# Feed-forward weights quantised and the rows of batches 0 to 11 normalised and transposed inside the first attention

## The reference

```python
x = x + jnp.tanh(g_xattn[0]) * _L0_xattn_ref(_layernorm(x, axis=-1), ctx_1024, ...)   # 16 heads of 64
x = x + jnp.tanh(g_ffn[0]) * _L0_ffn_ref(_layernorm(x, axis=-1), w_gate, w_up, w_down)

def _L0_ffn_ref(x, w_gate, w_up, w_down):
    x = act_qdq(x)                                # 16 bits, ONE scale: max |x| over all rows / 32767
    up = act_qdq(x @ lpbq_dequant(w_up).T)        # weights 4 bits, a scale for each 32 of a row
    gate = act_qdq(x @ lpbq_dequant(w_gate).T)
    sig = fixed_qdq_u16(jax.nn.sigmoid(gate))
    gate = act_qdq(gate * sig)
    o = act_qdq(gate * up)
    return o @ lpbq_dequant(w_down).T
```

## Time and profile before

| | |
|---|---|
| median of three runs | 1631.07 us (1628.36 to 1631.30) |
| profiled execution, its own time | 1624.04 us |
| its span | 1622.2 us |
| TensorE busy | 1399.8 us, 86% |
| DVE busy | 1230.6 us, 76% |
| ACT busy | 1103.1 us, 68% |
| GpSimd busy | 179.3 us, 11% |
| mean granted clock of TensorE | 0.936 |

### The profile page before, as it was taken

The page is one execution under the profiler, slowest core; times in us unless marked ns, Lnnn a source line. Parts: engine busy times, 40 slices in busy tenths (PEclk is TensorE's granted clock), DMA queues, the critical chain, the costliest instruction groups (busy, mean ns, idle before and its releaser), DMA issues. The chain is left out here.

```text
span 1622.2 us, 40480 instructions
## 1 busy us (share of the span) xinstructions
PE 1399.8 (86%) x15436; PEld 995.7 (61%) x15436; DVE 1230.6 (76%) x3108; ACT 1103.1 (68%) x2440; POOL 179.3 (11%) x177
## 2 busy tenths in 40 slices
PE   5899999999999993492379898989898689999996
PEld 3577666666667662340366666666666367788884
DVE  5888888888888877758778999898898877344443
ACT  5777777777777763467428889888888654366663
POOL 1000001100000002200000000000000100034443
PEclk9999999999999997797688999999999889999998
DMA  6122232332322211000011121211010072122221
GB/s 206 46 86 85 85 107 90 96 107 85 98 93 91 76 60 59 0 1 26 0 57 50 54 77 54 77 51 28 18 35 12 21 251 68 56 35 46 49 45 23
DMA packets 64924, 105.67 MB, mean 65 GB/s; under 512 B 7449, under 2 KB 38914, under 8 KB 63586
## 3 DMA queue, kind: packets, MB, share of 16 engines
q1 hardware_dynamic: 58018, 94.83, 18.6%
q0 software_dynamic: 6720, 8.27, 3.2%
HBM read 68.88 MB, written 35.11 MB: 64 GB/s over the span
## 5 line engine op out<-in xcount | busy, mean ns | idle before, releaser
L1482 ACT ACTIVATE a_p<-a_s,a_nb 112x375 f32<-112x375 f32 x256 | 140.9, 598 | 26.5 <-DVE a_nb L1585 26.2
L271 PE MATMUL a_ps_o<-a_vh,a_pt 125*128 125x64 f16 (+1 forms) x1536 | 152.8, 183 | 2.6 <-ACT a_pt L1495 0.8
L1402 PE MATMUL a_ps_t<-ident,a_p 112*128 112x112 f32 x768 | 118.1, 284 | 42.6 <-ACT a_p L1482 41.3
L273 PE MATMUL a_ps_o<-a_vh,a_pt 125*128 125x64 f16 (+1 forms) x1536 | 151.1, 182 | 0.0
L272 PE MATMUL a_ps_o<-a_vl,a_pt 125*128 125x64 f16 (+1 forms) x1536 | 151.0, 182 | 0.0
L618 ACT ACTIVATE a_p<-a_ps_s,a_nb 112x375 f32<-112x375 f32 x256 | 144.0, 573 | 2.7 <-DVE a_scaled L768 2.1
L271 PEld LDWEIGHTS a_ps_o<-a_vh,a_pt 125*128 125x128 f16 x1536 | 133.5, 98 | 14.7 <-ACT a_pt L1495 6.4
L626 ACT ACTIVATE a_pt<-a_ps_t 125x336 f16<-125x336 f32 x256 | 101.5, 448 | 59.4 <-PE a_ps_t L555 59.1
L1402 PEld LDWEIGHTS a_ps_t<-ident,a_p 112*128 112x128 f32 x768 | 79.6, 146 | 97.8 <-issue 82.7
L272 PEld LDWEIGHTS a_ps_o<-a_vl,a_pt 125*128 125x128 f16 x1536 | 130.8, 98 | 11.0 <-issue 0.2
L1585 DVE CUSTOM_DVE_ANT_0 a_s<-a_s,a_fill 112x375 f32<-112x375 f32 x256 | 130.3, 547 | 5.5
(11 more groups left out here) (443 smaller groups left out, 4486.7 us busy)
## 6 DMA issues: line engine op xcount, KB each, us to landing
a_piece<-in_w SPq DMA_DIRECT2D x72, 256.0 KB, 3.0
split_weights<-a_pair SPq DMA_DIRECT2D x72, 256.0 KB, 3.3
w<-split_weights SPq DMA_DIRECT2D x8, 1024.0 KB, 6.1
a_ctx<-in_ctxT SPq DMA_DIRECT2D x16, 375.0 KB, 3.6
ctx<-a_cx SPq DMA_DIRECT2D x16, 375.0 KB, 4.2
a_cx<-ctx SPq DMA_DIRECT2D x16, 375.0 KB, 5.9
w1h<-split_weights SPq DMA_DIRECT2D x2, 1792.0 KB, 14.8
w1l<-split_weights SPq DMA_DIRECT2D x2, 1792.0 KB, 18.0
```

The source lines that it names most:

```text
L271: nc.tensor.matmul(out, wh, mh, start=(i == 0), stop=False)
L273: last = nc.tensor.matmul(out, wl, mh, start=False, stop=(i == n - 1))
L1402: mm = nc.tensor.matmul(ps_t[:, 2 * (g % 2) + i, t * S:(t + 1) * S], p32[:, g % 2, i, t * KV:t * KV + 128], ident32[0:S, 0:S], start=(t == ...
L1482: nc.scalar.activation(p32[:, g % 2, i, 0:NC], s2[:, g % 2, i, :], ACT.Exp, bias=nb[:, g % 2, i:i + 1], scale=-1.0).then_inc(exp_done, 1)
```

## The change

- `norm_phase` and `WeightQuantiser` go, and with them the block.
- `xh` and `xl` become one tile `x16` with the two halves of a group of four batches side by side, so that the room of a group (`row_floats`) can hold the normalised rows in fp32 once the attention's queries are done with it. `of_batch` gives a batch's columns.
- The weights are quantised in six parts i of 768 columns in the attention: `block_scales` in slot 2, `block_steps` in slot 3 and `block_values` in slot 6 of the batches 2, 3, 5, 6, 7 and 10, all on DVE (GpSimd and ACT had a part of it before), and 14 T jobs in slots 3 and 6 of batches 3, 4, 6, 7, 8, 10, 11 and 12. SP loads part i in its iteration `QUANT_AT[i]` - 1 into the room of the attention's weight stage, two parts deep.
- `bn_stats` of the finished row b - 1 stands in slot 5 of batch b. The rows of batches 0 to 11 are normalised from batch 13 on (`FLAT_ROW_AT`), with six N jobs (`FLAT_AT`), whose results stay fp32; DVE finds the largest of each.
- The feed-forward's own block begins with the last four rows, the largest of all, the all-reduce and the scale; then ACT rounds to 16-bit integers, and DVE makes the two fp16 halves, a cast and a subtraction for each part of a group, 16 in all; TensorE starts as soon as the first group is split.

```diff
+        QUANT_AT = {0: 2, 1: 3, 2: 5, 3: 6, 4: 7, 5: 10}
+        T_AT = {(3, 3): ("T0", 0), (3, 6): ("T1", 0), (4, 3): ("T0", 1), (4, 6): ("T1", 1), (6, 3): ("T0", 2),
+                (6, 6): ("T1", 2), (7, 3): ("T0", 3), (7, 6): ("T1", 3), (8, 3): ("T0", 4), (8, 6): ("T1", 4),
+                (10, 3): ("T2", 4), (11, 3): ("T0", 5), (11, 6): ("T1", 5), (12, 3): ("T2", 5)}
+        FLAT_AT = {NP * b + p: (f"N{k}", n) for n, (b, ps2) in enumerate(((14, (1, 2)), (14, (7, 8)), (15, (5, 6))))
+                   for k, p in enumerate(ps2)}
+        FLAT_ROW_AT = {NP * b + p + i: TG * n + i for n, (b, p) in enumerate(((13, 4), (14, 3), (15, 1))) for i in range(TG)}
...
+            def load_quant(i):
+                src, o = quant_source(i)
+                if i == 0:
+                    sp.wait_ge(w_lo, len(loads))
+                if i >= 2:
+                    sp.wait_ge(q_rounded, i - 1)
+                sp.dma_start(raw[:, i % 2, :].rearrange("p (o d) -> p o d", o=o), src).then_inc(q_in[i % 2], 16)
+
             for b in range(B):
                 sp.wait_ge(ctx_lo, b + 1)
                 if b + 1 < B:
                     sp.dma_start(ctx32[:], A["ctxT"][:, :, (b + 1) * NC:(b + 2) * NC].rearrange("k p n -> p k n")
                                  ).then_inc(ctx_in, 16)
+                for i in QUANT_AT:
+                    if b == QUANT_AT[i] - 1:
+                        load_quant(i)
                 wait(sp, ctx_kept, 16 * b)
...
+                if g == NP * 13 + 1:
+                    roots(3, 0, B - TG)
...
+            def block_scales(i):
+                r = i % 2
+                dve.wait_ge(q_in[r], 16 * (i // 2 + 1))
+                stat(nc.vector.tensor_reduce(block_max[:, r], blocks(raw[:, r]), AX.X, ALU.max, apply_absolute_value=True))
+                stat(nc.vector.tensor_scalar(block_scale[:, r], block_max[:, r], 1.0 / 7.0, 1e-12, ALU.mult, ALU.max))
+                nc.vector.reciprocal(block_inv[:, r], block_scale[:, r]).then_inc(q_scaled, 1)
+
+            def block_steps(i):
+                r = i % 2
+                dve.wait_ge(q_scaled, i + 1)
+                nc.vector.tensor_tensor(blocks(steps[:, r]), blocks(raw[:, r]), spread(block_inv[:, r]), ALU.mult
+                                        ).then_inc(q_rounded, 1)
+
+            def block_values(i):
+                r = i % 2
+                dve.wait_ge(q_rounded, i + 1)
+                if i >= 2:
+                    dve.wait_ge(job_done, NUMBER[LAST_T[i - 2]] + 1)
+                nc.vector.scalar_tensor_tensor(out=blocks(whole[:, r]), in0=blocks(steps[:, r]), scalar=7.0,
+                                               in1=spread(block_scale[:, r]), op0=ALU.min, op1=ALU.mult
+                                               ).then_inc(q_whole, 1)
...
                 if g in ROW_AT:
                     normalise_row(ROW_AT[g])
+                b, p = divmod(g, NP)
+                if 1 <= b and p == 5:
+                    dve.wait_ge(job_lo, NUMBER["W", b - 1] + 1)
+                    nc.vector.bn_stats(row_stats[:, b - 1, :], x_res[:, b - 1, :]).then_inc(row_done, 1)
+                for i in QUANT_AT:
+                    if b == QUANT_AT[i] and p in (2, 3, 6):
+                        {2: block_scales, 3: block_steps, 6: block_values}[p](i)
+                if g == NP * 13:
+                    dve.wait_ge(row_done, B - TG)
+                    variances(0, B - TG, row_stats)
+                if g == NP * 13 + 3:
+                    reciprocal_roots(3, 0, B - TG)
+                if g in FLAT_ROW_AT:
+                    flat_row(FLAT_ROW_AT[g])
                 for i in slot_pieces(g):
                     split_low(i)
...
+            for t in range(TG):
+                nc.vector.tensor_scalar(xn[:, t, :], x_res[:, LAST + t, :], mv[:, t, 0:1], rstd[:, t:t + 1], ALU.subtract,
+                                        ALU.mult).then_inc(normed, 1)
+            for k in range(KD):
+                c = KD * (NG - 1) + k
+                dve.wait_ge(x_turned, k + 1)
+                nc.vector.tensor_reduce(largest0[:, c:c + 1], pj[:, k, 0:GW], AX.X, ALU.max, apply_absolute_value=True
+                                        ).then_inc(x_found, 1)
+            dve.wait_ge(x_found, KD)
+            nc.vector.tensor_reduce(mx[:, 7:8], largest0[:], AX.X, ALU.max).then_inc(x_max, 1)
+            dve.wait_ge(x_max_all, 1)
+            link(nc.vector.tensor_scalar(sx[:], am[:, 7:8], 1.0 / QMAX, 1e-12, ALU.mult, ALU.max))
+            nc.vector.reciprocal(inv[:], sx[:]).then_inc(x_scaled, 1)
+            for g in range(NG):
+                for k in range(KD):
+                    dve.wait_ge(x_rounded, KD * g + k + 1)
+                    nc.vector.tensor_copy(xh[:, k, g, :], x_int[:, k, g, :]).then_inc(x_high, 1)
+                for k in range(KD):
+                    dve.wait_ge(x_high, KD * g + k + 1)
+                    nc.vector.tensor_tensor(xl[:, k, g, :], x_int[:, k, g, :], xh[:, k, g, :], ALU.subtract
+                                            ).then_inc(x_split, 1)
```

More of the change, by code:

```diff
@@ L318, in attention0_phase @@
         piece, pair = sb("a0_piece", [128, 3, CH]), sb("a0_pair", [128, 4, 2 * CH], F16)
+        room = flat(stage[:])
+        QC = 3 * D
+        raw, whole = (room[:, i * 2 * QC:(i + 1) * 2 * QC].rearrange("p (r n) -> p r n", r=2) for i in range(2))
+        steps = room[:, 4 * QC:5 * QC].bitcast(I16).rearrange("p (r n) -> p r n", r=2)
+        block_max, block_scale, block_inv = (sb(f"a0_{n}", [128, 2, QC // QBLK]) for n in ("bmax", "bscale", "binv"))
         ps_s = ps("a0_ps_s", [128, 2, 512])
@@ L335, in attention0_phase @@
         x_in = [sem(f"a0_x_in{i}") for i in range(2)]
+        q_in = [sem(f"a0_q_in{i}") for i in range(2)]
         piece_in = [sem(f"a0_piece_in{i}") for i in range(3)]
@@ L380, in attention0_phase, with quant_source, quant_result @@
         assert sorted(PIECE_SLOT) == list(range(PIECES))
+        def quant_source(i):
+            m, half = divmod(i, 2)
+            if m < 2:
+                return (A[("L0_ffn_w_up", "L0_ffn_w_gate")[m]][half * 384:(half + 1) * 384].rearrange("(o p) d -> p o d", p=128),
+                        3)
+            return A["L0_ffn_w_down"].rearrange("(o p) d -> p o d", p=128)[:, :, half * 384:(half + 1) * 384], KD
+        def quant_result(k, i):
+            m, half = divmod(i, 2)
+            w = weights0[m]
+            if m < 2:
+                return [w[:, a, k, half * 384:(half + 1) * 384] for a in range(2)], [o * D + k * 128 for o in range(3)]
+            return [w[:, a, 3 * half + k, :] for a in range(2)], [o * 384 + k * 128 for o in range(KD)]
+        LAST_T = {i: ("T1" if i < 4 else "T2", i) for i in range(6)}
         def where(i):
@@ L491, in project @@
                                                    ident32[0:S, 0:S])
+                elif name[0] == "N":
+                    k = int(name[1])
+                    for i in range(TG):
+                        last = nc.tensor.transpose(ps_j[:, bank, i * S:(i + 1) * S], xn[:, i, k * 128:(k + 1) * 128],
+                                                   ident32[0:S, 0:S])
+                elif name[0] == "T":
+                    to, at = quant_result(int(name[1]), b)
+                    for i, c in enumerate(at):
+                        last = nc.tensor.transpose(ps_j[:, bank, i * 128:(i + 1) * 128], whole[:, b % 2, c:c + 128],
+                                                   ident32[:])
                 elif name[0] == "O":
@@ L832, in _ @@
             stat(statistics(0, TG))
-            variances(0, TG)
+            variances(0, TG, stats)
             low("K0", 0)
@@ L937, in _ @@
                 w = (wgt, wup)[m]
+                if n < NJ and o == 0:
+                    pe.wait_ge(x_split, KD * (g + 1))
                 wait(pe, copied, n - 5)
@@ L2390, in program @@
         own, neg16 = sb("own", [128, 2]), sb("neg16", [128, 128], F16)
[L2392 removed]
+        x16 = sb("x16", [128, KD, NG, 2, GW], F16)
+        xh, xl = (x16[:, :, :, i, :] for i in range(2))
         rows = nc.dram_tensor("normed_rows", (T, D), F32, kind="Internal").ap()
```

386 lines of the change are left out of this document (112 added, 274 removed).

## The result

The changed kernel takes 1614.3 us (median of five runs, 1612.45 to 1616.03). The kernel before, run beside it, takes 1628.36 (median of five, 1622.47 to 1631.30). The ratio is 0.9918, with a 95% interval of 0.9890 to 0.9945: faster by 0.8%. The forecast was 1621.8. The profiled execution of the changed kernel took 1614.3 us, 9.7 less than the 1624.04 of before; the forecast had 9.3 less, 1614.7. The two medians here lie further apart, 14.1; the other rounds of the kernel before have medians of 1624.2 and 1625.5, 10 to 11 above 1614.3.

A forecast was written before the change was run, and what follows sets the result against it. DVE carried nearly all of the 50.7 us feed-forward block while TensorE stood still for 37.96. Won 38.1 less 28.8 paid takes 9.3 off the profiled 1624.04, 1614.7; with the median 7.0 above, 1621.8, range 1602 to 1634.

The forecast's parts named there:

- The front: Feed-forward's start, up to TensorE's first gate product: 10.0 us instead of 50.7, so 40.7 won.
- The clock: Gate stage after TensorE's pause: 5.1 us at half speed lose 2.6, leaving 38.1 won.
- SP's queue: Attention, batch 5: `load_quant(4)` waits for `block_steps(2)`, holding up pieces; TensorE 7.3 late plus 2.0 for clock, 9.3 (6.5 to 11).
- `bn_stats`: End of slot 5 in every batch, where nothing is free: 0.33 each less 0.03, 14 times, 4.2 (0 to 5).
- `block_steps` and `block_values`: Attention slots 3 and 6: steps cost 0.7 or 0.6 a batch, 3.1 (0 to 5.4); values nothing.
- T jobs: Attention, TensorE's transposes: 0.4 for jobs of three, 0.3 for jobs of two, 5.0 in all.
- N jobs of batch 14: Attention, TensorE: four jobs at 0.5 each for four transposes, as for X jobs, 2.0.
- Batch 13: Attention: table switch pair 1.5, variances in slot 0 0.5, reciprocals in slot 3 0.6; 2.6 (1.5 to 5).
- Batch 15: End of the attention, a chain through the exponentials: two maxima, a statistics step and rows cost 2.0.
- The first: Rival: only TensorE's columns and table loads count, SP's wait and DVE's work hide; 10.6 paid, 1603.6; chance 0.22.
- The second: Rival: DVE bounds the attention's slots; its 41 us land on the path, 53 paid, 1646; chance 0.13.
- The third: Rival: nearly cancels; SP's stall at upper bound, values and scales half exposed, all-reduce 2.7; 1631; chance 0.13.

The follow-up runs named there:

- experiment 8: Against the kernel of experiment 1, identity transposes keep TensorE busy through the feed-forward's front; execution 1604.8 us against 1601.5, sigmoid's table load 3.10 us earlier after the last taking.
- experiment 1: Against the changed kernel, SP takes `load_quant(4)` one batch later, in iteration 7 instead of 6; 1603.11 us, ratio to before 0.9871.
- Experiment 9: Against the kernel of experiment 1, N jobs moved to batch 14 slots 3, 4 and batch 15 slots 0, 1, group 1's rows one slot later; two periods together -2.08 us.

## Why the prediction was right, point by point

- **The front.** 10.0 was forecast, 9.75 measured; 40.7 won, 40.9 measured. The all-reduce took 0.38 by GpSimd's row and DVE waited 0.55 for it, so the lower of the two rows of before was the right one to take. It is the first all-reduce of its program, so the 2.71 was no price of a first use. In the kernel before DVE was at work beside it, from before its start until 0.24 before its end at 661.29:

```profile
658.36 2.69 DVE L1182 TENSOR_SCALAR qw_q<-qw_q 128x1536 f32<-128x1536 f32 x3
```

By the SBUF — State Buffer page of the Trainium skill (SBUF: two separate sides) the 2.71 would be a wait for DVE. The two rows fit that, 2.71 beside a working DVE and 0.38 beside a waiting one; no run here varies DVE's work alone.
- **The clock.** 5.1 us at half speed were forecast for 2.6, and 5.4 were seen. Between the first gate product (10.05 earlier than before) and the sigmoid's table load (7.40 earlier) 2.65 are lost, and experiment 8 shows TensorE's idle time to be the cause. The two loads, before first:

```profile
715.90 1.28 ACT L967 ACT_TABLE_LOAD   x1
```

```profile
708.50 1.28 ACT L942 ACT_TABLE_LOAD   x1
```

- **SP's queue.** The step with the longest working held: 9.3 forecast, 9.29 measured by experiment 1. Its parts held as well: 7.46 of lateness and 1.83 for the clock were measured, 7.3 and 2.0 forecast.
- **`bn_stats`.** Forecast 4.2, 0.30 each; measured 0.17 each, 2.4. The step that failed is "nothing is free" in slot 5, read from one weight load that had stood for `a_otl`; 0.25 of each was free. It is a size and not the mechanism: moved out of the slot, the cost is gone.
- **`block_steps` and `block_values`.** Forecast 3.1 and 0; together 0.70 in batch 2 (0.61 in batch 10), six times that 4.2, one of which the forecast had left to the stall. Steps in slot 3 do cost something, 0.18 to 0.30 more than in slot 4 in five of six batches, while a second `block_values` costs its whole length. How the 0.70 divides between the two can't be told from these runs.
- **`block_scales`.** Forecast 0. It delays slot 2 of batch 2 by 1.42 and most of that is given back. Periods 0 and 8, which hold it with a `bn_stats` alone, fall back to those of before once the `bn_stats` stands in another slot, so there it costs nothing; periods 3 and 5, which hold T jobs as well, are 0.35 and 0.19 longer than their other parts add up to, but so are periods 2 and 6, without scales, by 0.13. Whether scales and T jobs lean on each other stays open.
- **T jobs.** Forecast 5.0. T0 and T1 together cost 0.65 (periods 7 and 10 less a `bn_stats`), six times 3.9; T2 shows nothing in period 9. About 1 too high.
- **N jobs of batch 14.** Forecast 2.0, measured 2.66 in slots 1 and 2 and about 1.0 in slot 7 and the one behind: 3.7. The term priced them like X jobs, by TensorE's columns; the row for X jobs stood in slots with two or three jobs, and the first two N jobs in slots with four. Experiment 9 shows the place to be the cause.
- **Batch 13.** Table pair 1.5 forecast, 1.44 measured; variances 0.5 forecast, 0.8 measured (2.42 less 0.17 and 1.44). The ScalarE: Activation LUTs page of the Trainium skill (What ACT_TABLE_LOAD costs) would have added 2.8 here. The measured pair leaves no room for that. The page's 1283 ns for the load itself agree with the rows, 1.28; its drain does not show in them, the root starts at 537.51 where the load from 536.22 ends at 537.50.
- **Batch 15.** Forecast 2.0. The changed kernel shows 1.82, which looks like a hit and is none: the work costs 0.15, and a clock drop of 1.67, which the step did not have, fills the rest.
- **The sum.** 28.8 forecast against 28.1 for what the change does. Of the single terms `bn_stats`, batch 15 and the T jobs were too high by 1.8, 1.9 and 1.1, the N jobs and steps with values too low by 1.7 and 1.1, and the misses cancelled for the most part: that the sum is off by only 0.7 is in part luck. Not foreseen were 1.7 for the clock drop at the attention's end, 1.1 at the start of the program, which is chance (the first taking lies between 87.57 and 90.38 in the twelve kernels with this start), and 2.4 given back behind the gate stage, where the clock was higher than before in two places. These cancel too, so the agreement of 9.7 with 9.3 is closer than its parts. Windows of the down product and of the second attention's start, changed kernel first, the kernel before second:

```profile
785.00:800.00 15.00, 11.86 (x94) 11.86 (x95) 7.59 (x15) 12.65 (x12) 0.00 (x0) 0.78 0.00 0
...
845.00:870.00 25.00, 22.18 (x309) 15.04 (x308) 22.61 (x66) 22.31 (x41) 2.93 (x4) 0.98 0.19 57
```

```profile
792.00:807.00 15.00, 11.48 (x80) 11.48 (x81) 6.40 (x14) 12.64 (x12) 0.00 (x0) 0.69 0.00 1
...
852.00:877.00 25.00, 22.98 (x274) 15.70 (x272) 18.99 (x58) 18.87 (x36) 2.93 (x4) 0.79 0.07 18
```

- **The number.** 1621.8 is 7.5 above the 1614.3 measured, and nearly all of it is the base. The step that failed is the last one, in which the difference was put on a median of three runs 7.0 above the profiled execution. The runs of the kernel before beside the experiments gave 1624.2 (median of seven), 1625.5 (median of eleven) and once 1621.7, all near the profiled 1624.04.
- **The rivals.** The first is out (1603.6): SP's stall was real, though without it the kernel does take 1603.1, by another sum. The second did not come about, but its mechanism did at the margin: every further microsecond of DVE costs one. The third is out: the all-reduce was short and SP's stall not at its upper bound. Two sums in them were slightly off: the second turns the change to a loss from 26 of its 41, not 29, once the 2.6 of ACT are counted, and the third adds up to 1632.5, not 1631.

## What to carry to other kernels

A request that waits for a buffer belongs into its queue at the point where the buffer is free, not where the order of the data suggests: one such request, taken a batch too early, gave back nearly a quarter of what the front won (9.3 of 40.9). DVE, busy 84 of 100 us before the change, hid only the first of what was added to it, 0.25 of 0.42 us and 1.2 of 1.9, and then nothing; so price an addition by what already stands in its slot and in the two behind it, and put it beside few jobs, not fourth in a chain of two banks. Where a program repeats to 0.02 us, a mark that recurs prices single instructions from one profile; medians can't.

## What was not expected of the hardware

- The clock's drops after short idle times are not the same from run to run of like code: the last period of the attention was 24.14 (three of twelve) or 25.5 to 26.0 (nine), slot 3 of batch 15 5.43 or 6.90, and a whole stretch of the second attention had 1.00 or 0.56. Together they move a run by more than most of the edits here.
- After the stall in the attention TensorE worked at 0.50, and after a front of 10 us with 1.8 us of work likewise; filled with transposes that front stayed at 1.00.
- The partition all-reduce took 0.38 us, with a wait of 0.55 for DVE, where the first one before had taken 2.71.
